# One-hots stored once by the first message layer and loaded by the five later ones, turned one-hots in fp32 alone

## The reference, cut to what matters

```
logit[e, h] = f(row[src[e]], row_dst[dst[e]])         # dot product, or leaky_relu(a + b), ...
p[e, h]     = exp(logit[e, h] - max over edges of dst[e])
acc[n, h]  += sum over edges e with dst[e] == n of  p[e, h] * row[src[e], h]   (and of p itself)
```

## Time and profile before

| | |
|---|---|
| median of 3 runs | 7668.35 us (7663.28 to 7670.11) |
| span of the profiled execution | 8869.1 us; the page gives no other time for this execution |
| busy in it: PE, DVE, ACT, POOL | 5045.4 (57%), 4591.5 (52%), 5330.2 (60%), 5197.0 us (59%) |
| DMA | 744.58 MB, 84 GB/s over the span |
| largest groups on POOL | 5124 indirect gathers, 5056.6 us |

### The profile page before, as it was taken

The page is one execution under the profiler, slowest core; times in us unless marked ns, Lnnn a source line. Parts: engine busy times, 40 slices in busy tenths (PEclk is TensorE's granted clock), DMA queues, the critical chain, the costliest instruction groups (busy, mean ns, idle before and its releaser), DMA issues. The chain is left out here.

```text
span 8869.1 us, 129245 instructions
## 1 busy us (share of the span) xinstructions
PE 5045.4 (57%) x21094; PEld 3760.6 (42%) x21094; DVE 4591.5 (52%) x15579; ACT 5330.2 (60%) x14791; POOL 5197.0 (59%) x5195
## 2 busy tenths in 40 slices
PE   3888887445565635555634444554555554556555
PEld 2444444333343423433423444443544553455554
DVE  3666666434444634444533333364565555455555
ACT  1777777256666646666636666663666664566666
POOL 3556563266666466666556666635666663566664
PEclk7999999767666767666755555566777776677777
DMA  2222222134444334444322222201222222333342
GB/s 67 73 73 73 74 75 50 48 107 115 111 113 113 92 112 113 114 111 113 110 70 71 69 71 69 68 14 47 69 67 67 67 67 66 99 110 109 110 110 83
DMA packets 428332, 744.58 MB, mean 84 GB/s; under 512 B 207788, under 2 KB 248113, under 8 KB 427439
## 3 DMA queue, kind: packets, MB, share of 16 engines
q0 software_dynamic: 205312, 519.10, 23.0%
q1 hardware_dynamic: 218976, 215.57, 8.2%
q10 hardware_dynamic: 3280, 1.64, 0.1%
HBM read 718.36 MB, written 17.56 MB: 83 GB/s over the span
## 5 line engine op out<-in xcount | busy, mean ns | idle before, releaser
L476 POOL DMA_INDIRECT gat_ring<-tab,gat_ixb x2562 | 2579.9, 1007 | 1371.9 <-issue 769.0
L820 PE MATMUL gat_sc_ps<-gat_ring,gat_oh 128*128 128x264 f32 (+1 forms) x5124 | 1809.0, 505 | 600.4 <-issue 389.2
L820 PEld LDWEIGHTS gat_sc_ps<-gat_ring,gat_oh 128*128 128x128 f32 x5124 | 1184.6, 276 | 792.0 <-issue 656.8
L476 POOL DMA_INDIRECT conv_ring<-tab,conv_ixb x854 | 812.1, 951 | 655.3 <-issue 335.3
L476 POOL DMA_INDIRECT dot_ring<-tab,dot_ixb x854 | 833.1, 976 | 596.6 <-issue 272.1
L920 ACT ACTIVATE gat_oh<-gat_off,one 128x256 f32<-128x256 bf16 x1281 | 636.4, 497 | 857.2 <-PE gat_sc_ps L820 247.1
L476 POOL DMA_INDIRECT gatv_ring<-tab,gatv_ixb x854 | 831.5, 974 | 511.2 <-issue 237.9
L618 DVE TENSOR_TENSOR acc<-acc,gat_sc_ps 128x264 f32 (+1 forms) x1281 | 489.8, 382 | 1140.0 <-PE gat_sc_ps L820 318.2
L900 ACT ACTIVATE gat_off<-iota,rel 128x128 bf16<-128x128 f32 x2562 | 868.0, 386 | 0.1
L914 ACT ACTIVATE gat_ohT<-gat_offT,one 128x256 bf16<-128x256 bf16 x1281 | 633.9, 495 | 384.7 <-issue 271.2
L609 DVE TENSOR_TENSOR gat_ring<-gat_ring,gat_p_sb 128x520 f32<-128x520 f32 (+1 forms) x1281 | 769.6, 601 | 4.1
(11 more groups left out here) (455 smaller groups left out, 9991.0 us busy)
## 6 DMA issues: line engine op xcount, KB each, us to landing
gat_rel_row<-d_rel SPq DMA_DIRECT2D x216, 384.0 KB
gat_ring<-tab,gat_ixb POOLq DMA_INDIRECT x2562
conv_rel_row<-d_rel SPq DMA_DIRECT2D x72, 384.0 KB
gatv_rel_row<-d_rel SPq DMA_DIRECT2D x72, 384.0 KB
dot_rel_row<-d_rel SPq DMA_DIRECT2D x72, 384.0 KB
conv_ring<-tab,conv_ixb POOLq DMA_INDIRECT x854
conv_ring<-in_attr SPq DMA_DIRECT2D x427, 32.0 KB
gatv_ring<-tab,gatv_ixb POOLq DMA_INDIRECT x854
```

The source lines that it names most:

```text
L476: gp.indirect_dma_start(out=ring[:, r, t, 0:width], out_offset=None, in_=table[:, :], in_offset=bass.IndirectOffsetOnAxis(ap=ixb[:, r, t:t ...
L820: last = pe.matmul(sc_ps[:, m % SCB, 0:F], oh[:, m % 4, u, :], rows, start=(u == 0), stop=(u == 1))
```

## The change

In `conv` every one-hot is stored to DRAM when it has been made; the five later layers load all of them and make none.

- Two DRAM tensors hold them, both fp32, in batches of four groups (`RG` goes from 6 to 4): each batch is one block of 128 partitions x 4 KB.
- In `conv`, `ohT`, `oh` and `offT` get three buffers (`OHB`). For each group SP issues two more DMAs of 128 partitions x 1 KB: `keep_turned` after `ohT`, and `keep_plain` after `oh`. ACT writes an `ohT` buffer only after the store of the group three before has landed, and DVE an `oh` buffer likewise. SP's order changes: `numbers` for two batches and the attributes of the first three chunks come first, then for each position `keep_turned`, `keep_plain`, and the attributes of the next chunk.
- In the five other layers `rel_row`, `offT`, `off`, `ohT` and `oh` are gone. SP issues for each four groups one load of turned and one of plain one-hots (512 KB each) into two buffers each. A buffer is filled again when PE has used up the batch in it. ACT has no one-hots to make.
- The gat layers' expansion keeps its bf16 matmul and reads the upper half of each fp32 word, a step of two bf16 elements.

```diff
-RG = 6
+RG = 4
 RB = 2
+OHB = 3
...
+            def keep_turned(n):
+                b = n % OHB
+                sp.wait_ge(s("ohT"), n + 1)
+                sp.dma_start(one_group(T.d_turned, n), ohT[:, b].rearrange("p u e -> p (u e)")
+                             ).then_inc(s(f"turned_out{b}"), 16)
+
+            def keep_plain(m):
+                sp.wait_ge(s("oh"), m + 1)
+                sp.dma_start(one_group(T.d_plain, m), oh[:, m % OHB].rearrange("p u e -> p (u e)")
+                             ).then_inc(s(f"plain_out{m % OHB}"), 16)
+
+            def turned_in(k):
+
+                behind(sp, s("ex"), RG * (k - RB + 1))
+                n = min(RG, NGR - RG * k)
+                sp.dma_start(turned[:, k % RB, 0:n].rearrange("p g u e -> p (g u e)"),
+                             T.d_turned[k, :, 0:n * GE]).then_inc(s(f"turned_in{k % RB}"), 16)
+
+            def plain_in(k):
+
+                behind(sp, s("scat"), RG * (k - RB + 1))
...
+            if conv:
+                for k in range(RB):
+                    numbers(k)
+                for ch in range(RING):
+                    for g in range(SIZES[ch]):
+                        attributes(ch, ch, g)
+            for i in range(NCH + 2):
+                for g in range(GC):
+                    n = BASE[i] + g if i < NCH and g < SIZES[i] else None
+                    m = BASE[i - 2] + g if i > 1 and g < SIZES[i - 2] else None
                     if conv:
-                        attributes(ch, ch % RING, g)
...
+                        if n is not None:
+                            keep_turned(n)
+                            if n % RG == RG - 1 and RG * (n // RG + RB) < NGR:
+                                numbers(n // RG + RB)
+                        if m is not None:
+                            keep_plain(m)
+                            if i + 1 < NCH and g < SIZES[i + 1]:
+                                attributes(i + 1, (i + 1) % RING, g)
+                    else:
+                        if n is not None and n % RG == 0:
+                            turned_in(n // RG)
+                        if m is not None and m % RG == 0:
+                            plain_in(m // RG)
+                    if gat and g == 0 and 0 < i <= NCH:
+                        landed(i - 1)
...
             def one_hot(i, g):
                 m = BASE[i] + g
+                behind(v, s("scat"), m - OHB + 1)
+                if m >= OHB:
+                    v.wait_ge(s(f"plain_out{m % OHB}"), 16 * (m // OHB))
...
+                    which = turned[:, n // RG % RB, n % RG]
+                    if gat:
+                        which = which.rearrange("p u e -> p (u e)").bitcast(BF16).rearrange(
+                            "p (u e w) -> p u e w", u=2, w=2)[:, :, :, 1]
...
+                a.wait_ge(s("offT"), n + 1)
+                behind(a, s("ex"), 2 * (n - OHB + 1))
+                if n >= OHB:
+                    a.wait_ge(s(f"turned_out{n % OHB}"), 16 * (n // OHB))
```

More of the change, by code:

```diff
@@ L418, in message_pass @@
     mx_ps = ph.ps("mx_ps", [P, 512])
-    if not conv:
-        off = ph.sb("off", [P, 2, 2, P], BF16)
     if gatv2:
@@ L517, in _ @@
-            if gat:
-                landed(NCH - 1)
+            if conv:
+                for k in range(RB):
[7 more added lines that the diff above has]
+                    m = BASE[i - 2] + g if i > 1 and g < SIZES[i - 2] else None
+                    if conv:
+                        if n is not None:
[6 more added lines that the diff above has]
+                                attributes(i + 1, (i + 1) % RING, g)
+                    else:
+                        if n is not None and n % RG == 0:
[4 more added lines that the diff above has]
+                        landed(i - 1)
+                if i == RING and own_to is not None:
+                    for j in range(NG):
+                        own_rows(j, own_to)
@@ L525, in _ @@
             for b in range(RB):
-                sp.wait_ge(s(f"rel_in{b}"), 16 * len(range(b, -(-NGR // RG), RB)))
+                batches = len(range(b, -(-NGR // RG), RB))
+                if conv:
+                    sp.wait_ge(s(f"rel_in{b}"), 16 * batches)
+                else:
+                    sp.wait_ge(s(f"turned_in{b}"), 16 * batches)
+                    sp.wait_ge(s(f"plain_in{b}"), 16 * batches)
             if conv:
+                for b in range(OHB):
+                    for out in ("turned_out", "plain_out"):
+                        sp.wait_ge(s(f"{out}{b}"), 16 * len(range(b, NGR, OHB)))
                 for b in range(SLOTS):
@@ L794, in expand @@
                         at = t % 12 * 24
-                        last = pe.matmul(ex_ps[:, t // 12, at:at + 24], ohT[:, n % OHB, u, :], mine, start=True, stop=True)
+                        last = pe.matmul(ex_ps[:, t // 12, at:at + 24], which[:, u, :], mine, start=True, stop=True)
                     last.then_inc(s("ex"), 1)
@@ L808, in expand @@
                         pe.nop(nofuse=True)
-                        pe.matmul(ex_ps[:, 2 * (n % 2) + u, 0:F], ohT[:, n % OHB, u, :], mine, start=True, stop=True
+                        pe.matmul(ex_ps[:, 2 * (n % 2) + u, 0:F], which[:, u, :], mine, start=True, stop=True
                                   ).then_inc(s("ex"), 1)
@@ L813, in scatter @@
                 m = BASE[i] + g
-                pe.wait_ge(s("oh"), m + 1)
+                if conv:
+                    pe.wait_ge(s("oh"), m + 1)
+                    which = oh[:, m % OHB]
+                else:
+                    if m % RG == 0:
+                        pe.wait_ge(s(f"plain_in{m // RG % RB}"), 16 * (m // RG // RB) + 16)
+                    which = plain[:, m // RG % RB, m % RG]
                 pe.wait_ge(s("msg"), m + 1)
@@ L819, in scatter @@
                     rows = msgs[:, m % 2, u, :] if conv else ring[:, r, 2 * g + u, W - F:W]
-                    last = pe.matmul(sc_ps[:, m % SCB, 0:F], oh[:, m % 4, u, :], rows, start=(u == 0), stop=(u == 1))
+                    last = pe.matmul(sc_ps[:, m % SCB, 0:F], which[:, u, :], rows, start=(u == 0), stop=(u == 1))
                 last.then_inc(s("scat"), 1)
@@ L976, in step @@
                 for g in range(GC):
-                    one_hots(i, g, g < read, g < summed)
+                    if conv and g < read:
+                        turned_one_hot(i, g)
                     if conv and g < summed:
```

67 lines of the change are left out of this document (26 added, 41 removed).

## The result

The changed kernel takes 7705.91 us (median of 4 runs, 7690.77 to 7711.94), the kernel before 7666.1 beside it: 1.0047 times, 95% interval 1.0033 to 1.0061, so about 40 us (0.5%) slower. The forecast was 7688, slower by 20.

What follows compares the result with a forecast made beforehand. POOL's gathers were taken to bound at least the five later layers, leaving 103 us of 7668 for POOL's waits. Later layers -5, store loop +15 and conv's start +8 gave +18; 7688 with a little for DMA jitter, range 7655 to 7735.

Steps and rivals of the forecast that it cites:

- the crawl: Profiled execution: other engines' instruction handling slows while POOL issues gathers; taken as recording's weight, absent from measured runs.
- after 240 us of the trace: Sign that would show the forecast: conv's first sum comes later than this; it was at 231 before.
- if the crawl were real: Conv's start, worse case: attribute loads end near 229 us, first sum near 260, costing +30.
- Later layers, -5: Five later layers: without ACT's one-hots, the last two chunks' drain shortens 1 us a layer; bounds 0 and -15.
- Conv, +23: First layer's total cost: +8 us for its start and +15 for its store loop.
- +8: Conv's start: 36 attribute loads before the first store delay ACT; expansions end at 175 us, near 167 before.
- +15: Conv's store loop: ACT's wait for the turned store, 2.30 us a group, up to 2.91; upper bound 68 us.
- same upper bound: Conv: DVE's new wait for the plain store, costed 0, with the turned store loop's 68 us as limit.
- Step-two read and loads, 0 each: Later layers: PE's every-second-element bf16 weight loads, and SP's loads of one-hots, lie off the path and cost nothing.
- B: Rival: ACT does hold the later layers; -86 us there, 7600 with conv's +18; chance 0.20.
- C: Rival: the store loop binds conv, with three buffers and SP behind a wait; +68, 7754 us; chance 0.15.
- D: Rival: DMA engines crowd in the first two gat layers and dot; 260 us, half taken, 7818; chance with E 0.13.

Runs made afterwards that it cites:

- stores only: First layer of the changed kernel, storing its one-hots; later layers of the kernel before, making their own: 7699.69 us against 7675.09, 1.0032.
- turned stores only: Against the kernel whose first layer stores both one-hots and whose later layers make their own: plain one-hots no longer stored; 8912.83 us, 1.0035.
- half as many loads again: Changed kernel, loading 256 KB once more per batch of both tiles in all later layers but dot: 8827.50 us, 0.9944 of the kernel before.
- ScalarE's copies: ACT instead of DVE weights gathered rows in the later layers: on the changed kernel 8874.55 us; with late attribute loads and four buffers 8977.68, then 7525.86.
- the kernel with four buffers: Changed kernel with late attribute loads and four buffers, not three, for each first-layer one-hot: 8794.70 us (0.9906 of the kernel before), again 8921.34 (0.9894).
- late attribute loads: Changed kernel with only the first chunk's 12 attribute loads ahead of the first store, the others between the stores: 7693.10 us, 1.0024 of the kernel before.

## Why the prediction was right, and where it wasn't

**What bounds the kernel.** Right, and it carried the forecast: the sum of gathers and 0.30 us gaps left 103 us for POOL's waits, and a trace at the right pace shows 107, all in conv. That the two agree so well is luck. The sum took its terms from a trace of the slow kind of chip; the right one has 932.6 us outside the layers and not 971.3, 5072.0 us of gathers and not 5056.6, and gaps of 0.305 us in the later layers and not 0.30. These move what is left for waits by +39, -15 and -20 us, and so nearly cancel. With the multiplication moved to ACT, the gathers of the five later layers became 204.3 us shorter in all and the layers 203.5 us, so there the gathers do set the pace. ACT's busy share of 69% bounded nothing.

**Why the profile was 15.7% long.** Wrong. I took the crawl to be the weight of recording. In the experiments all runs of the kernel before took 8866 us or more on two chips, and 7662 to 7685 on two others, its profiled one (7673.84) too: the crawl goes with the chip, or with the occasion, for no chip was met twice. By its span the first profile is of the one kind; the first times are of the other. The sum survived because it was made against the measured time. What follows from the wrong reason was wrong: the first sum "after 240 us of the trace" came at 187.9, and that the "span may move by much more" has nothing to do with what is recorded. The branch "if the crawl were real" (attribute loads out near 229, first sum near 260, +30) is what the slow kind does: 230.4 and 269.5 us, 38 later than before.

**Later layers, -5.** The size was off, by a little: 5557.7 us before and 5553.4 with stores only, and 5557.9, 5563.5, 5564.2 and 5568.1 in four traces with loads, +6 to +10 on average. All of it is in gatv2 and dot (1088.7 to 1091.9 and 1085.1 to 1087.9 us with loads, 1082.4 to 1084.0 and 1081.9 to 1083.8 without), 2 to 11 ns a gather; the wide gat layers don't change. I said gathers wouldn't lengthen, and named it as a sign of being wrong; at this size it is one for the term, not for the mechanism. The wide layers' gathers, at 1.04 us, lie above my 1.03 too, but before as after. Traffic by itself isn't the cause, as far as the runs show: on the slow kind `gatv2`'s gathers took 831.8 us with turned stores only, 836.9 with loads and 837.8 with half as many loads again, and with ScalarE's copies `dot`'s fall to 0.95 us beside 210 GB/s. The cause stays open. The -5 was to come from the last two chunks, which lie in the stretches outside: 925.9, 929.2, 932.5 and 934.1 us in those four traces, 932.6 and 935.6 in two without loads. The means differ by 4, which is within what two traces of one kernel differ by (925.9 and 929.2 are both the changed kernel's).

**Conv, +23.** Measured 23.2: start 11.0 for +8, store loop 11.9 for +15. The attribute loads took 41.3 us where I had 36.4, the fourth turned one-hot came at 152 for 147, and the 21 expansions, which I had end at 175, were done only before the first sum, at 188, since PE waits for ACT and DVE between them. In the store loop the wait that shows is DVE's, for the plain store, which I had costed at nothing with "same upper bound" because the sum that waits for the add comes two periods later. The logits are queued behind it as well, and PE's expansion waits for them. So the +15, made of the turned store's loop, was near the total for a reason that it doesn't give: that is luck. That the turned store hardly showed and the plain one did is read from the traces with three buffers; no run takes away one of the two alone on this kind of chip, and on the other kind the plain store is worth 6 to 10 us of conv.

**The parts together**: 23 + 6 = 29 us, about 25 with the 4 outside. The traces' spans differ by 17 and 26 (7688.9 and 7697.8 against 7672.1), the medians by 40 and 35, where the kernel before alone spreads over 20. The 10 to 15 us between aren't placed.

**Step-two read and loads, 0 each.** Right: PE is busy 569 us in the first gat layer, 599 before, and the DMA share is 0.63 (0.45 before at this pace) where 0.69 was estimated. The weight loads that read every second bf16 element take as long as those of the kernel before; shortest, median and longest in ns, after and before:

```profile
L859 PEld LDWEIGHTS gat_ex_ps<-nd,gat_turned x672: 96/98/152, 1711.5 to 2597.4; 128*128 128x128 bf16 x168
```

```profile
L795 PEld LDWEIGHTS gat_ex_ps<-nd,gat_ohT x660: 95/98/152, 1701.5 to 2599.1; 128*128 128x128 bf16 x165
```

**The rivals.** B falls here, since POOL has no gap for ACT to cause; on the other kind of chip the later layers do shrink, by 87 us, as far as argued through ACT's instructions. That its price was 86 is chance: it was five sixths of 103 us of waits, and there POOL waits 968 us in the later layers. There the changed one-hots win: the kernel with four buffers is 0.9% and 1.1% faster than the kernel before, and the changed kernel with extra loads, the nearest to the changed kernel itself that ran there, 0.56%. C is true in kind, but at 12 us, not 68. D falls: 198 GB/s here and 222 there, without longer gathers in the wide layers. What the Trainium skill, SBUF — State Buffer, section Who interferes with whom, says of DMA and of VectorE's second SBUF input agrees with these runs, but for the 2 to 11 ns in `gatv2` and `dot` that are open: the loads cost the wide layers' gathers nothing, and with the DVE instruction of two SBUF inputs taken away the gather's mean went from 1.04 to 0.95 us.

## What to carry to other kernels

Count what the pacing engine must do, its fixed gap included, against the measured time, not against the span of one profile; what is left is all that any other change can win. An engine that has been emptied is worth nothing by itself and much as a place for work that disturbs the pacing engine: the same change that lost 35 us was the ground for winning 140. (No run adds the copies to the kernel before; there ACT is already busy 796 of 1149 us in such a layer, and they would ask for 0.24 x 8 x 427 = 820 more.) When stores are added to a queue, look first at what is issued ahead of the first one, and have one buffer more than the steady sum asks for, as far as the memory allows.

## What the runs showed of the hardware

- Two kinds of chip, two of each seen: the kernel before takes 7662 to 7685 us on some and 8866 to 9029 on others. Gathers (0.94 us at least) and their gaps of 0.30 us are the same on both; the other engines crawl on the slow one while POOL issues gathers without a pause (SP takes 121.3 us for 36 DMA issues and not 41.3; PE's expansions stand 6 to 7 us apart and not 1.0). An edit's sign can differ: loading the one-hots, with late attribute loads and four buffers, gains 1% on the slow kind, where the plain change loses 0.4 to 0.5% on the fast one; adding ScalarE's copies takes 203.5 us from the fast kind's later layers and costs 56 us on the slow one. What makes the chips differ isn't shown, nor that the same chip would always be of one kind.
- An indirect gather of 128 rows costs POOL 0.94 us and 0.30 more to the next, whether a row is 128 or 264 floats; nearly all of its longer times in the wide layers went when DVE's multiplication of the rows, with two inputs in SBUF, was moved to ACT, while the loads stayed: 0.5 us on the gather shown, up to 1.9 on single ones (2.8 us in all), 0.09 on the mean.
- ScalarE's in-place copy with a scale takes 0.33 us for 65 columns, with the next one started 0.24 us after it, and the gathers beside it keep 0.95 us.
- A bf16 weight load of 128x128 that takes every second element costs PE no more than one of adjacent elements: 98 ns in the median either way.
